# Attention with a token-mixing tail on one core: transposes placed among the score passes in five slots, and two small transposes retyped to float32r

## What is computed

```python
q, k, v = jnp.einsum('bsx,xMnd->Mbnsd', x, qkv)
a = jnp.einsum('bnsd,bntd->bnst', q, k) * q.shape[-1] ** (-0.5)
cum = jnp.cumsum(rpe_bias[:, :s], axis=-1)
rel = jnp.arange(s)[:, None] - jnp.arange(s)[None, :]
bias = jnp.where(rel >= 0, cum[:, jnp.clip(rel, 0)], PAD)
a = jax.nn.softmax(a + bias, axis=-1)
mix = jnp.einsum('bnst,bntd->bnsd', a, v)
x = _layernorm(x + jnp.einsum('bnsd,ndx->bsx', mix, out_w), axis=-1)
```

## Time and profile before

| | |
|---|---|
| median of 3 runs | 1132.71 us (1132.38 to 1134.63) |
| profiled execution, its own time | 1129.46 us |
| its span, first to last instruction | 1127.7 us |
| PE busy (matmul) | 1066.2 us, 95% |
| weight loads (PEld) busy | 756.3 us, 67% |
| DVE busy | 807.2 us, 72% |
| ACT busy | 729.8 us, 65% |
| mean granted TensorE clock | 0.989 of full |

### The profile page before, as it was taken

One profiled execution on the slowest core, in us unless ns is written; L12 is line 12 of the kernel. 1 busy time (PEld: TensorE's weight loads), 2 busy tenths in 40 slices (PEclk: granted clock), 3 DMA queues, 4 the chain that ended last, 5 costly groups with the idle time before them and its releaser, 6 DMA issues.

```text
span 1127.7 us, 21564 instructions
## 1 busy us (share of the span) xinstructions
PE 1066.2 (95%) x6973; PEld 756.3 (67%) x6973; DVE 807.2 (72%) x2121; ACT 729.8 (65%) x1857; POOL 6.7 (1%) x16
## 2 busy tenths in 40 slices
PE   5899999999899999999989999999999999999994
PEld 4666666667576777676667676677666677767773
DVE  2766666767567778777768777778876778877756
ACT  3767666667566777676766676767666667667633
POOL 1000000000000000000000000000000000000000
PEclk9999999999999999999999999999999999999998
DMA  8865666576647676757667666677756766675710
GB/s 213 229 154 144 148 144 161 146 188 165 155 126 171 157 180 157 181 145 181 148 161 174 168 156 157 171 181 173 182 140 159 171 168 162 173 173 149 234 41 21
DMA packets 113005, 180.71 MB, mean 160 GB/s; under 512 B 13152, under 2 KB 69360, under 8 KB 112896
## 3 DMA queue, kind: packets, MB, share of 16 engines
q1 hardware_dynamic: 110736, 178.42, 63.5%
q10 hardware_dynamic: 2160, 0.92, 0.3%
HBM read 58.41 MB, written 20.22 MB: 70 GB/s over the span
## 4 chain that ended last, share of the span: by engine, by line
PE 76%; DVE 6%; issue 5%; ACT 4%; DMA 4%; SPq 4%; DVEq 0%; POOL 0%; ACTq 0%
PE ps_o L1026 22%; PE ps_rows L985 20%; PE ps_t L1002 11%; PE ps_m L960 7%; PE ps_m L965 4%; PE ps_m L1042 4%; DMA stacks<-k_lo 3%; PE ps_o L1002 3%; ACT prob L508 2%; SPq L305 2%; DVE prob L667 2%; DVE pt L691 2%; ACT pt L526 1%; PE ps_rows L1098 1%; DVE mix_sb L698 1%
## 5 line engine op out<-in xcount | busy, mean ns | idle before, releaser
L508 ACT ACTIVATE prob<-prob,low 128x128 f32<-128x128 f32 (+7 forms) x512 | 395.4, 773 | 104.5 <-DVE low L667 99.3
L667 DVE CUSTOM_DVE_ANT_0 prob<-ps_rows,table 128x128 f32<-128x128 f32 (+7 forms) x512 | 379.6, 749 | 52.3 <-PE ps_rows L985 35.7
L985 PE MATMUL ps_rows<-stacks 128*128 128x512 f32 (+3 forms) x1536 | 395.8, 369 | 16.1 <-DMA stacks<-k_lo 12.1
L1002 PE MATMUL ps_t<-ident_r,prob_r 128*128 128x128 f32 x1984 | 282.7, 262 | 11.8 <-ACT pt L526 5.0
L1002 PEld LDWEIGHTS ps_t<-ident_r,prob_r 128*128 128x128 f32 x1984 | 211.7, 141 | 96.2 <-issue 74.0
L985 PEld LDWEIGHTS ps_rows<-stacks 128*128 128x128 f32 x1536 | 245.8, 190 | 37.8 <-DMA stacks<-k_lo 13.0
L1026 PE MATMUL ps_o<-pt,v_pair 128*64 128x512 f32 (+3 forms) x1536 | 268.7, 492 | 0.0
L691 DVE COPY pt<-ps_t 128x256 f32<-128x256 f32 (+2 forms) x320 | 177.8, 564 | 108.6 <-PE ps_t L1002 108.2
L526 ACT ACTIVATE pt<-ps_t 128x512 f32<-128x512 f32 (+3 forms) x352 | 163.0, 463 | 88.5 <-PE ps_t L1002 87.8
L1026 PEld LDWEIGHTS ps_o<-pt,v_pair 128*64 128x64 f32 x1536 | 101.8, 136 | 176.1 <-issue 163.8
L960 PE MATMUL ps_m<-x_cur,w_cur 128*128 128x512 f32 x250 | 130.3, 603 | 2.8 <-DVE q_lo L653 1.6
(11 more groups left out here) (119 smaller groups left out, 608.8 us busy)
## 6 DMA issues: line engine op xcount, KB each, us to landing
stacks<-k_hi SPq DMA_DIRECT2D x126, 256.0 KB, 4.6
stacks<-k_lo SPq DMA_DIRECT2D x126, 256.0 KB, 5.1
inv_all<-inverse_sums SPq DMA_DIRECT2D x128, 128.0 KB, 3.4
stacks<-q_hi SPq DMA_DIRECT2D x63, 256.0 KB, 3.9
stacks<-q_lo SPq DMA_DIRECT2D x63, 256.0 KB, 4.4
mix_transposed<-mix_sb SPq DMA_DIRECT2D x62, 256.0 KB, 3.6
table<-bias_by_distance SPq DMA_DIRECT2D x64, 192.0 KB, 3.7
mix_tile<-mix_transposed SPq DMA_DIRECT2D x24, 512.0 KB, 4.7
```

The lines of the kernel that those rows point to most:

```text
L508: nc.scalar.activation(row, row, ACT.Exp, bias=low[:, r:r + 1], scale=-1.0, accum_out=total[:, r:r + 1]).then_inc(s_exp, 1)
L667: nc.vector.tensor_tensor_reduce(prob[:, r % PSLOTS, 0:width], ps_rows[:, score_at(r):score_at(r) + width], table[n % 2][:, h, 0:width][:, ...
L985: ins = nc.tensor.matmul(ps_rows[:, at + c0:at + c1], q_st(h, n)[:, P * i:P * i + P], k_st(h, n, low_part)[:, c0:c1], start=(low_part == 0 ...
L1002: ins = nc.tensor.transpose(t_bank[TBANK[k]][:, P * b:P * b + P].bitcast(F32R), prob_r[:, r % PSLOTS, at:at + P], ident_r[:, :])
```

## The change

The table AMONG names five slots. In these the blocks of the slot's transposes stand among the score passes of the row four ahead: after pass w of c come the blocks up to `blocks * (w + 1) // c`. What followed the scores in slots 9 and 10 (RK and the projection of v) now follows the transposes too. `score` issues one pass and `transpose` one block; their waits are as before. Aliases of the same addresses typed float32r are added for inv and x1, and their transposes use them with ident_r.

```diff
+AMONG = (6, 8, 9, 10, 14)
...
+        with nc.sbuf_tensor("inv_r", [P, NROWS], F32R) as inv_r:
+            pass
+        inv = sb("inv", [P, NROWS])
+        with nc.sbuf_tensor("x1_r", [P, C], F32R) as x1_r:
+            pass
+        x1 = sb("x1", [P, C])
...
+            def passes(r):
+
+                at, width = score_at(r), P * (ROWS[r][1] + 1)
+                cut = min(BANK - at % BANK, width)
+                return [(c0, max(c1, c0 + SHORTEST), low_part) for c0, c1 in ((0, cut), (cut, width)) if c0 < c1
+                        for low_part in range(2)]
...
+                if block == 0:
+                    pe.wait_ge(s_exp, NROWS * n + r + 1)
+                if block == b0:
...
-                        ins = nc.tensor.transpose(t_bank[TBANK[k]][0:2 * GROUP, 3 * P:],
-                                                  inv[:, 2 * GROUP * g:2 * GROUP * (g + 1)], ident[:, :])
+                        ins = nc.tensor.transpose(bank[0:2 * GROUP, 3 * P:],
+                                                  inv_r[:, 2 * GROUP * g:2 * GROUP * (g + 1)], ident_r[:, :])
...
-                        ins = nc.tensor.transpose(t_bank[TBANK[k]][:, P:2 * P], x1[:, :], ident[:, :])
+                        ins = nc.tensor.transpose(bank[:, P:2 * P], x1_r[:, :], ident_r[:, :])
...
-                    for row in rows_ahead(n, more, slot):
-                        score(*row)
+                    blocks = ROWS[slot][1] + 1
+                    moved = 0
+                    for m, row in rows_ahead(n, more, slot):
+                        count = len(passes(row))
+                        for which in range(count):
+                            score(m, row, which)
+                            share = blocks * (which + 1) // count if slot in AMONG else 0
+                            for block in range(moved, share):
+                                transpose(n, slot, block, tile_too)
+                            moved = max(moved, share)
...
-                    transpose(n, slot, tile_too)
+                    for block in range(moved, blocks):
+                        transpose(n, slot, block, tile_too)
```

More of the change, by code:

```diff
@@ L139, in build @@
         total = sb("total", [P, NROWS])
-        inv = sb("inv", [P, NROWS])
         inv_t = [sb(f"inv_t{g}", [2 * GROUP, P]) for g in range(2)]
@@ L149, in build @@
         o_tile = sb("o_tile", [P, C])
-        x1 = sb("x1", [P, C])
         x1_t = sb("x1_t", [P, 1 + SEQ])
@@ L967, in project @@
                 ins.then_inc(s_proj, 1)
-            def score(n, r):
-                h, i = ROWS[r]
[L972 to L993, removed]
+            def passes(r):
[3 more added lines that the diff above has]
+                        for low_part in range(2)]
@@ new lines, in score @@
+            def score(n, r, which):
+                h, i = ROWS[r]
+                if which == 0:
+                    if n == 0 and r == 0:
+                        pe.wait_ge(s_first, 96)
+                    elif i % GROUP == 0:
+                        pe.wait_ge(s_stack[h], 96 * n + 96)
+                    pe.wait_ge(s_biased, NROWS * n + r + 3 - rows_since(r))
+                c0, c1, low_part = passes(r)[which]
+                at = score_at(r)
+                ins = nc.tensor.matmul(ps_rows[:, at + c0:at + c1], q_st(h, n)[:, P * i:P * i + P],
+                                       k_st(h, n, low_part)[:, c0:c1], start=(low_part == 0), stop=(low_part == 1))
+                if which == len(passes(r)) - 1:
+                    ins.then_inc(s_score, 1)
@@ L995, in transpose @@
+            def transpose(n, r, block, tile_too):
+                k = next(k for k in range(NBANKS) if BANKS[k][0] == r and BANKS[k][1] == block // 4 * 4)
+                _, b0, nb = BANKS[k]
+                bank = t_bank[TBANK[k]].bitcast(F32R)
+                if block == 0:
+                    pe.wait_ge(s_exp, NROWS * n + r + 1)
+                if block == b0:
                     if TBANK[k] == 2 and 2 not in TBANK[:k]:
@@ L999, in transpose @@
                         pe.wait_ge(s_ev[engine], count)
[L1000 to L1003, removed]
+                ins = nc.tensor.transpose(bank[:, P * (block - b0):P * (block - b0) + P],
+                                          prob_r[:, r % PSLOTS, P * block:P * block + P], ident_r[:, :])
+                if block == b0 + nb - 1:
                     if k in INV_BANK:
@@ L1066, in _ @@
             for r in range(LEAD):
-                score(0, r)
+                for which in range(len(passes(r))):
+                    score(0, r, which)
             project(0, 4, False)
```

## The result

The changed kernel takes 1210.7 us (median of 4 runs, 1205.0 to 1214.7) against 1133.7 (4 runs) of the kernel before: a ratio of 1.068, 95% interval 1.065 to 1.071. The forecast was 1195, the range 1160 to 1212; two of the four runs, 1212.61 and 1214.69, lie just over its end. The profiled execution took 1212.61, so 83.1 more than the profiled 1129.5 of before.

The account below looks back on a forecast made before the run. PE bounds the kernel on average, but DVE has no slack in slots 6 to 10. 32 pairs × 2.3 = 74, less 8 of DMA waits and 3 of clock, gives +63: 1195 us, range 1160 to 1212.

Parts of the forecast that it names:

- The two gates: Row 9's and row 10's first transposes, in slots 9 and 10, wait for DVE's copies about 1.0 and 1.1 us.
- The price per pair: Slots 6 to 10: row 15's first load goes 2.3 us later in each of 32 pairs, 74 us in all.
- Slots 8 and 14: Extra switches between transposes and score passes there are hidden by waits that already exist, so they cost nothing.
- the retyping: float32r transposes of inv and x1: worth less than 2.6 us in all, either way; taken as 0.
- The weight loads behind passes: By the rows, 12 moved transposes a pair save nothing behind passes: 0.3 us longer, where the skill page implies 0.3 shorter.
- In pairs without a token tile RK is missing, but both gates are DVE's, so the loss is the same: Slots 9 and 10 of pairs without a token tile: the same 2.3 us loss as in the other pairs.
- What is given back: Later PE swallows 8 us of slot 12's 13.0 us of DMA waits; the clock kept up gives 3 us more.
- DVE's share: In slots 6 to 10 DVE's busy share falls from 100% to about 80%, with holes before biases of rows 13 and 14.
- Only the first gate: Rival: slot 10's wait stays hidden if DVE copies bank 10 soon enough; 1160 us, chance 0.10.
- A third gate on ACT: Rival: ACT's copy of v or its queue is 1 us late in 23 pairs with a tile; +23, 1218 us, chance 0.10.
- Fewer waits: Rival: interleaving fills PE's waits at row 8's fifth block and row 9's first transpose; 12 us faster, 1120, chance 0.06.
- No change: Rival: later waits make up all of PE's lateness, so the time stays the same; chance 0.02.

Follow-up runs that it names:

- the filler: The changed kernel plus two float32 matmuls (four passes, result unused) at RK's place in slot 9 of pairs without a token tile; 1197.1 us, ratio 1.059.

## Why the prediction was right, and where it was off

**The two gates: right.** Stands forecast at about 1.0 and 1.1 us, measured 1.06 and 1.27; holes in DVE at the biases of rows 13 and 14, the first forecast at 0.74 and measured at 0.66. The price per pair was 2.3 and is 2.4. The parts alone gave 0.2 for slot 6 (forecast 0.22), 0.9 for slot 9 and 1.4 for slot 10. The 0.1 too little holds for the pairs with a tile and is 0.1 × 23 = 2 us of the miss.

**Slots 8 and 14, and the retyping: right.** All three at 0; the runs alone gave 1.002 and 1.001, both within what a measurement tells.

**The weight loads behind passes: right to go by the rows.** A moved transpose gained nothing, neither in slot 8 nor in the whole.

**"In pairs without a token tile RK is missing, but both gates are DVE's, so the loss is the same": this step failed.** The gates are the same (2.3 in the run with the filler), but with RK missing between them PE's second stand is 1.72, and around its end the clock falls. I had looked at the clock only for what the shorter DMA waits would give back. The fall cost 11 to 14 us by the medians, most of the 15.7 by which the forecast was low, and 18 to 19 in the profiled executions, where the forecast was low by 20.1. No term of the sum and no end of the range was made for it: the range came from 20% on the 2.3. That the time still lies in it, 1.3 under its end, is in part luck, helped by the waits below.

**What is given back: waits too small, clock right.** I took 8 us of slot 12's waits and left two of about 2 us; 11.8 are gone, and one of 1.2 is left. With slot 9 alone 9.7 are left on the weight loads, with slot 10 alone 3.5, so the later PE is, the less is left. The longest wait, 4.11, stood in the last early pair. There the loads from row 8's first transpose to row 11's first span 8.5 us before and 12.7 after, the fallen clock in it, which is enough to swallow the wait whole; with the filler they span 11.2, and 0.99 is left. So the failed step above also made this term too small. The 4.06 one, in a pair with a tile, shrank by 3.0 where the pair is 2.4 longer; why it is more stays open. The clock came back where I expected it: on the mean of 7 us it was 0.56 and 0.76 behind the two long waits (from 309.40 and 581.10), and in the same places of the changed kernel (from 345.30 and 631.40) it is 1.00. Whether that is worth the 3 us that I took no run shows apart.

**DVE's share** fell to 83% where I wrote about 80.

**The rivals.** Only the first gate: slot 10 alone cost more than slot 9. A third gate on ACT: it is there, but L1052's load (L1062 after) stands for the copy of v only 0.19 us, and pairs with a tile are 0.1 longer than forecast, not 1. Fewer waits: two were made and none taken away; the one at row 8's fifth block grew from 0.27 to 0.40. No change: of the 95 us that the pairs lost, only slot 12's 11.8 and the clock behind two of these waits came back.

## What to carry to other kernels

On an engine that takes its work in order, a step that waits may stand ahead only of steps that nobody waits for; ask of each moved wait what is then behind it, and who needs that. Here a transpose that needs an engine's copy was put ahead of the passes which that engine needs next, so both stood in turn, 2.3 us a pair. The work that stood in front of such a wait was cover, and where it is missing (the pairs without a tile), ask what PE's clock does behind the longer stand: here that was a fifth of the loss in the profiled execution, and four matmul passes whose result nobody reads got it back.

## What was not expected of the hardware

In the early pairs the clock fell the more often, the longer PE's two stands were together, and four passes between them kept it up. The last column counts the early pairs whose 10 us from row 9's gate on had a mean clock of 0.83 or 0.66; in all others it was 0.98 to 1.00.

| run | stands at row 9 and row 10 | pairs of nine |
|---|---|---|
| before | 0.49 and 0 | 0 |
| slot 9 alone | 1.06 and 0.12 | 0 |
| transposes behind all passes | 0.49 and 0.79 | 0 |
| slot 10 alone | 0.48 and 1.36 | 4 |
| change, bank 6 to ACT | 0.63 and 1.72 | 4 |
| change | 1.06 and 1.72 | 9 |
| change with filler | 1.06 and 1.27, 0.45 of work more | 0 |

The table has the stands of most early pairs; the first pair's stand at row 9 is shorter in most runs (0.63 in the change). The runs don't separate how much of the filler's effect is the shorter stand and how much the work.

Nor does a stand's length alone tell what follows. Behind the wait of 2.27 us in the kernel before the clock was 1.00. With slot 10 alone, slot 12's load stood 1.74 us twice, in two pairs with a tile:

```profile
605.00 0.30 PEld L992 LDWEIGHTS ps_rows<-stacks 128*128 128x128 f32 x2 [1.74 <-DMA stacks<-k_lo]
...
883.60 0.30 PEld L992 LDWEIGHTS ps_rows<-stacks 128*128 128x128 f32 x2 [1.74 <-DMA stacks<-k_lo]
```

```profile
605.00:612.00 7.00, 6.93 (x50) 6.45 (x51) 4.18 (x15) 4.69 (x15) 0.00 (x0) 0.76 0.31 91
883.60:890.60 7.00, 6.83 (x61) 6.52 (x62) 4.29 (x17) 5.65 (x17) 0.00 (x0) 1.00 0.37 103
```

The first was followed by a fallen clock and the second, in the same slot, was not. What decides between them no run shows.
